# Sending the bf16 parts of q and k to DRAM in three steps instead of one, in a fused two-layer transformer block

## The chip, the cores and the metric

One Trainium2 chip, one core. The metric is the device time of one execution in microseconds (us). The change is written in Bass: every engine has an instruction list of its own, in a fixed order, and waits are semaphore waits written by hand.

## The reference

The input is x of 16 batches x 512 tokens x 128 channels in f32. Four residual layers follow one another, each with a layer norm in front (scale and shift free):

```
x = x + attention0(layernorm(x))     # 16 heads of 8, q, k, v with bias, softmax(q k^T / sqrt(8)) v, then wo
x = x + gated_mlp(layernorm(x))      # silu(x wg) * (x wu), 384 wide, then wd; weights from int8 ranges
x = x + attention1(layernorm(x))     # 16 heads of 8, q and k RMS-normalised per head, softmax, projection
x = x + moe_lora(layernorm(x))       # base linear + softmax-gated sum of 8 rank-8 experts, times 2
```

Per batch and attention layer there are 16 heads x 512 x 512 scores, each a dot product over 8 numbers only.

## The kernel before, in words

**The attention trick.** A score's dot product is over 8 numbers in f32. The kernel splits each f32 q and k into three bf16 parts (part 0 = q rounded to bf16, part 1 = the rest rounded, part 2 = the rest of that) and multiplies six pairs of parts (`Q_PART`, `K_PART`), so that 8 x 6 = 48 rows of bf16 stand for one head's f32 product. Two more rows hold the negated row maximum in two bf16 parts, so that the exponential needs no separate subtraction. To get parts, heads and terms onto the right partitions, the parts go through DRAM: SP writes `q_rows` and `k_rows` (L437), three DMAs for each of q and k, for terms 0 to 2, 3 and 4, and 5; then SP reads them back, four heads' worth at a time, into `q_stack` and `k_stack` (L452).

**Where the parts are made.** ScalarE (ACT) takes q and k out of PSUM (`take_qk`, L771) and makes part 0 (`take_part0`, a copy on L718, tiles qp and kp). GpSimd (POOL) makes part 1 (L602, then L604 updates the rest) and part 2 (L610). Semaphores `part0`, `resid1` and `part2` tell of them. ACT may overwrite part 0 only when the last batch's rows have landed (`rows_out`).

**Staging.** The kernel is one software pipeline. Every (layer, batch) attention is a slot of 64 units; there are 32 slots, in the order (0,0), (0,1), (0,2), (1,0), (0,3), (1,1), (0,4), (1,2), ... In each unit t TensorE (PE) makes one attention score tile (`attend_score`, L1237), one tile for the row maxima of the attention 26 units later (`max_score`, L1227), and each fourth unit four probability-times-value products (L1252). VectorE (DVE) reduces the maximum tile (L973), ACT takes the exponential (L742). Everything else (norms, projections, the MLP) is hung into this grid at units given in tables (`PE_AT`, `ACT_AT`, `DVE_AT`, `POOL_AT`, `SP_AT`): a name, and a unit counted from a slot's start. PE's tiles are handed PSUM banks from two rings: `A_RING` (banks 0, 1, 2, 7: all scores, all maxima and most pieces) and `V_RING` (3, 4, 5: two pieces, `xt3` and `kt`); bank 6 collects the attention output.

**The tables set order, not time.** Each engine walks the units in order and does what is due. SP has no work of its own in a unit: it runs ahead until a wait stops it, and all that is listed later waits behind that. SP's work, by its due units in a slot: `rows0` to `rows3` (`max_rows`, L458: two small DMAs that put the maxima of a quarter into `q_stack`; attention score 16n of the slot waits for quarter n), `den`/`rden` (L464, L472, L478: softmax denominators out and their reciprocals back in), `lx` (`load_x`, L418: the input of a later batch, which DVE reads first, L949), `lr0`, `cpx2`, `store`, `half0`/`half1` (`stack_half`, L452), and `out_p0`/`out_p1` (`parts_out`, L437: all six row DMAs of layer 0's or layer 1's next batch, three after q's part 2 is there and three after k's).

**Where the rows stand.** For layer 0 and batches 3 to 15 the group `P0` is used (`out_p0` at unit 47 of the slot of (0, b-1), 8 later for b = 3), for batches 1 and 2 the group `P0_fast` (unit 17; for b = 2, unit 19). Batch 0 goes ahead of the loop. Layer 1 has `out_p1` at unit 21 of the slot before (1, b), in most cases shifted 2 earlier. When two things are due in the same unit, their order in SP's loop decides.

Of the kernel before, what the change touches and what calls it, by code (L numbers as in the profile page):

```python
# [12 lines left out]
BATCH, SEQ, D = 16, 512, 128  # L13
# [11 lines left out]
PARTS = 3  # L25
TERMS = 6
Q_PART = (0, 0, 0, 1, 1, 2)
K_PART = (0, 1, 2, 0, 1, 0)
# [47 lines left out]
SP_AT = {"A": {"rows0": -5, "rows1": 9, "rows2": 32, "rows3": 43, "den0": 40, "rden0": 52, "den1": 71,  # L76
                "rden1": 74},
         "P0": {"out_p0": 47, "half0_p0": 72, "half1_p0": 95},
         "P0_fast": {"out_p0": 17, "half0_p0": 37, "half1_p0": 60},
         "S0": {"lx": 16},  # L80
         "M1": {"lr0": 52},
         "M2": {"out_p1": 21},
         "H1": {"cpx2": -16, "half0_p1": 38, "half1_p1": 42},
         "H1_tail": {"cpx2": 45, "half0_p1": 35, "half1_p1": 66},
         "E": {"store": 91}}
# [32 lines left out]
PE_DUE, ACT_DUE, DVE_DUE, POOL_DUE, SP_DUE = (due_table([t]) for t in (PE_AT, ACT_AT, DVE_AT, POOL_AT, SP_AT))  # L118
# [5 lines left out]
def at(due, name, t):  # L124

    return due[name][t] if name in due and t in due[name] else None
# [72 lines left out]
def build(nc, T, out_dram):  # L199
    ctx = ExitStack()  # L200
    with ctx:
# [7 lines left out]
        q_rows = [nc.dram_tensor(f"q_rows{l}", (128, TERMS, SEQ), BF16).ap() for l in (0, 1)]  # L209
        k_rows = [nc.dram_tensor(f"k_rows{l}", (128, TERMS, SEQ), BF16).ap() for l in (0, 1)]  # L210
# [173 lines left out]
        def _(sp):  # L384
            def hold(sem, value):
                need(sp, sem, value)
# [37 lines left out]
            load_res0(0)  # L424
            load_x(1)

            def parts_out(l, which, b):

                for n in which:
                    rows, pick = ((q_rows[l], Q_PART), (k_rows[l], K_PART))[n]  # L430
                    for h in (0, 1):
                        hold(stack_in[l][h], 64 * b)
                    hold(first_in[l], 64 * b)
                    hold(part2[2 * l + n], b + 1)
                    for j0, j1 in ((0, 3), (3, 5), (5, 6)):
                        step = pick[j0 + 1] - pick[j0] if j1 - j0 > 1 else 0
                        sp.dma_start(rows[:, j0:j1, :],  # L437
                                     bass.AP(qp[l][n][:, :, :].tensor, pick[j0] * SEQ,
                                             [[PARTS * SEQ, 128], [step * SEQ, j1 - j0], [1, SEQ]])
                                     ).then_inc(rows_out[l][n], 16)  # L440

            def stack_half(l, half, b):
                for n in (0, 1):
# [47 lines left out]
                sp.dma_start(out_dram[b:b + 1].rearrange("a (t p) d -> p (a t) d", p=128), x3[:, :, :]  # L491
                             ).then_inc(stored, 16)

            parts_out(0, (0, 1), 0)
            hold(k_ones, 1)
            stack_half(0, 0, 0)
            stack_half(0, 1, 0)
            for t in TIMES:
                b = at(SP_DUE, "half1_p0", t)
                if b is not None:  # L500
                    stack_half(0, 1, b)
                b = at(SP_DUE, "lx", t)
                if b is not None:
                    load_x(b)
                a = at(SP_DUE, "den1", t)
                if a is not None:
                    den_lines(a[0], 1, a[1])
                a = at(SP_DUE, "rows1", t)
                if a is not None:
                    max_rows(a[0], 1, a[1])  # L510
                a = at(SP_DUE, "rden1", t)
                if a is not None:
                    rden_lines(a[0], 1, a[1])
                b = at(SP_DUE, "lr0", t)
                if b is not None and b + 1 < BATCH:
                    load_res0(b + 1)
                b = at(SP_DUE, "out_p1", t)
                if b is not None:
                    parts_out(1, (0, 1), b)
                a = at(SP_DUE, "rows2", t)  # L520
                if a is not None:
                    max_rows(a[0], 2, a[1])
                b = at(SP_DUE, "half0_p1", t)
                if b is not None:
                    if b == 0:
                        hold(k_ones, 2)
                    stack_half(1, 0, b)
                b = at(SP_DUE, "half1_p1", t)
                if b is not None:
                    stack_half(1, 1, b)  # L530
                b = at(SP_DUE, "out_p0", t)
                if b is not None:
                    parts_out(0, (0, 1), b)
                a = at(SP_DUE, "den0", t)
                if a is not None:
                    den_lines(a[0], 0, a[1])
                a = at(SP_DUE, "rows3", t)
                if a is not None:
                    max_rows(a[0], 3, a[1])
                b = at(SP_DUE, "cpx2", t)  # L540
                if b is not None:
                    copy_x2(b)
                b = at(SP_DUE, "half0_p0", t)
                if b is not None:
                    stack_half(0, 0, b)
                a = at(SP_DUE, "rden0", t)
                if a is not None:
                    rden_lines(a[0], 0, a[1])
                a = at(SP_DUE, "rows0", t)
                if a is not None:  # L550
                    max_rows(a[0], 0, a[1])
                b = at(SP_DUE, "store", t)
                if b is not None:
                    store(b)
# [849 lines left out]
```

## Time and profile before

| | us |
|---|---|
| median of 3 runs | 1800.41 |
| lowest, highest run | 1794.83, 1801.01 |
| the profiled execution, its own time | 1797.05 |
| span in its profile, first to last instruction | 1795.3 |
| mean granted TensorE clock | 0.982 of full |
| PE busy | 1684.5 (94%) |
| DVE busy | 1543.6 (86%) |
| ACT busy | 1415.8 (79%) |
| POOL busy | 586.6 (33%) |
| DMA, 16 engines, mean share of the SP queue | 27.6% |

The profile tells of one execution. Times in its rows count from the first instruction. A timeline row has start, length, engine, source line, tiles written and read, a count when neighbours are merged, and in brackets the idle time just before it with what ended it. SPq rows are DMA issues: their length is the time SP spends on issuing, not the transfer. PEld rows are TensorE's weight loads, at which a score's wait shows.

### The profile page before, as it was taken

The numbers are of one execution on the slowest core, as the hardware profiler recorded it, in microseconds if no ns is written. First come the engines' busy times: TensorE is split into PE (matmuls) and PEld (weight loads), VectorE is DVE, ScalarE is ACT, GpSimd is POOL, SyncE is SP. The second block draws the span as 40 slices with busy tenths as digits, with TensorE's granted clock in tenths as the row PEclk, the third lists the DMA queues.
The fourth block names the chain that finished last, engine by engine and source line by source line (L and its number), as shares of the span: only waits on it lengthen the run. The fifth ranks groups of instructions, "written<-read, shape, count | busy, mean of one in ns | idle before, by whom it ended". The sixth has DMA issues, their size and how long they took to land.

```text
span 1795.3 us, 32451 instructions
## 1 busy us (share of the span) xinstructions
PE 1684.5 (94%) x10962; PEld 633.9 (35%) x10962; DVE 1543.6 (86%) x3347; ACT 1415.8 (79%) x2922; POOL 586.6 (33%) x840
## 2 busy tenths in 40 slices
PE   5999999999999999999999999999999999999995
PEld 2233333434333343333334333343433334334333
DVE  4988899898898989889898989989899898887981
ACT  2778788787978878787887988878797887777872
POOL 4224234151423324233242423415142332423311
PEclk8899999999999999999999999999999999999996
DMA  5232414223142322404232140422314142122310
GB/s 121 67 85 71 116 38 120 68 83 104 32 121 55 121 61 73 114 27 129 58 114 66 56 128 24 120 71 79 104 32 120 55 121 55 46 59 78 87 36 25
DMA packets 164024, 140.97 MB, mean 79 GB/s; under 512 B 40778, under 2 KB 145428, under 8 KB 163860
## 3 DMA queue, kind: packets, MB, share of 16 engines
q1 hardware_dynamic: 162084, 137.92, 27.6%
q8 instruction: 88, 1.44, 0.3%
q10 hardware_dynamic: 1776, 0.98, 0.2%
q14 instruction: 76, 0.62, 0.1%
HBM read 76.99 MB, written 55.57 MB: 74 GB/s over the span
## 4 chain that ended last, share of the span: by engine, by line
PE 62%; DVE 29%; issue 3%; ACT 2%; DMA 2%; SPq 1%; POOL 1%; DVEq 0%; ACTq 0%; POOLq 0%
DVE neg_max L973 20%; PE ps L1252 19%; PE ps L1237 14%; PE ps L1227 8%; PE ps L1273 7%; PE ps L1184 5%; PE ps L1266 3%; PE ps L1317 3%; DVE bn L949 2%; PE ps L1278 2%; DVE x L1010 2%; PE ps L1323 2%; DVE neg_high L979 1%; ACT probs L742 1%; DVE mv L957 1%
## 5 line engine op out<-in xcount | busy, mean ns | idle before, releaser
L973 DVE TENSOR_REDUCE neg_max<-ps 128x1 f32<-128x512 f32 x2048 | 1299.8, 682 | 100.2 <-PE ps L1227 91.1
L742 ACT ACTIVATE probs<-ps 128x512 f32<-128x512 f32 x2048 | 1093.3, 600 | 232.7 <-PE ps L1237 230.4
L1227 PE MATMUL ps<-k_stack,q_stack 48*128 48x512 bf16 x2048 | 679.1, 388 | 42.9 <-DVE neg_max L973 31.9
L1237 PE MATMUL ps<-q_stack,k_stack 50*128 50x512 bf16 x2048 | 632.1, 383 | 7.6 <-ACT probs L742 3.1
L1252 PE MATMUL ps<-probs,v_aug 128*32 128x512 f32 x4096 | 548.5, 608 | 0.7 <-ACT o_raw L718 0.7
L1237 PEld LDWEIGHTS ps<-q_stack,k_stack 50*128 50x128 bf16 x2048 | 148.1, 94 | 530.0 <-ACT probs L742 249.4
L1227 PEld LDWEIGHTS ps<-k_stack,q_stack 48*128 48x128 bf16 x2048 | 153.4, 93 | 227.4 <-DVE neg_max L973 202.1
L595 POOL TENSOR_TENSOR rstd<-vpe,half_neg 128x4 f32<-128x4 f32 x64 | 64.5, 1009 | 351.6 <-DVE vpe L964 351.5
L647 POOL TENSOR_TENSOR ht<-up,gs 128x512 f32<-128x512 f32 x48 | 61.1, 1273 | 223.2 <-ACT up L718 223.2
L1252 PEld LDWEIGHTS ps<-probs,v_aug 128*32 128x32 f32 x4096 | 80.7, 108 | 143.2 <-issue 73.7
L748 ACT ACTIVATE xn<-x,shift,rstd 128x128 f32<-128x128 f32 x192 | 80.7, 486 | 37.8 <-POOL shift L597 37.8
L616 POOL TENSOR_TENSOR o_raw<-o_raw,rden_all 128x512 f32<-128x512 f32 x64 | 81.3, 1270 | 49.9 <-DMA rden_all<-rden_rows 49.4
L602 POOL TENSOR_TENSOR qp<-qf,qp 128x512 bf16<-128x512 f32 x32 | 37.0, 1157 | 165.0 <-ACT qp L718 165.0
L654 POOL TENSOR_TENSOR coef<-gating,rm 128x64 f32<-128x64 bf16 x64 | 16.7, 292 | 225.3 <-DVE gating L1073 225.3
L1278 PE MATMUL ps<-wo,o_raw 128*128 128x128 f32 x512 | 67.3, 286 | 8.7 <-POOL o_raw L616 7.9
L626 POOL TENSOR_TENSOR nw_t<-nw_y 128x128 f32<-128x128 f32 x48 | 19.1, 399 | 156.2 <-DVE nw_y L1045 153.8
L1278 PEld LDWEIGHTS ps<-wo,o_raw 128*128 128x128 f32 x512 | 61.2, 196 | 18.3 <-issue 12.0
L1022 DVE SCALAR_TENSOR_TENSOR gs<-th,ps 128x512 f32<-128x512 f32 x48 | 32.7, 682 | 35.3 <-POOL ht L647 35.3
L1184 PE MATMUL ps<-ident,xn 128*128 128x128 f32 x256 | 44.1, 298 | 17.1 <-ACT xn L748 16.7
L718 ACT ACTIVATE up<-ps 128x512 f32<-128x512 f32 x48 | 28.7, 597 | 37.0 <-PE ps L1273 36.9
L1273 PE MATMUL ps<-xnt,w_up 128*128 128x256 f32 x192 | 54.3, 405 | 0.5 <-DVE gs L1022 0.5
L1010 DVE TENSOR_TENSOR x<-ps,x 128x512 f32<-128x512 f32 x32 | 22.0, 688 | 37.3 <-PE ps L1317 21.6
(117 smaller groups left out, 1579.5 us busy)
## 6 DMA issues: line engine op xcount, KB each, us to landing
rden_all<-rden_rows SPq DMA_DIRECT2D x64, 256.0 KB
q_rows<-qp SPq DMA_DIRECT2D x32, 384.0 KB, 2.9
k_rows<-kp SPq DMA_DIRECT2D x32, 384.0 KB, 2.9
q_stack<-q_rows SPq DMA_DIRECT2D x64, 192.0 KB, 3.8
k_stack<-k_rows SPq DMA_DIRECT2D x64, 192.0 KB, 4.8
q_stack<-q_rows SPq DMA_DIRECT2D x64, 144.0 KB, 2.9
k_stack<-k_rows SPq DMA_DIRECT2D x64, 144.0 KB, 3.3
q_rows<-qp SPq DMA_DIRECT2D x32, 256.0 KB, 3.1
```

What stands on the lines that cost most here:

```text
L595: pool.tensor_tensor(rstd[k][:, :], vpe[k][:, :], half_neg[:, :], ALU.pow).then_inc(rstd_ready[k], 1)
L616: pool.tensor_tensor(o_of(l, b)[:, c, :], o_of(l, b)[:, c, :], rden_all[:, c, :], ALU.mult).then_inc(att_ready[l], 1)
L647: pool.tensor_tensor(ht[:, c, :], up[:, :], gs[:, :], ALU.mult).then_inc(ht_done, 1)
L742: act.activation(probs[:, g % RING, :], home("score", (l, b, u)), ACT.Exp).then_inc(exps, 1)
L748: last = act.activation(xn[k][:, t, :], x[:, t, :], ACT.Identity, bias=shift[k][:, t:t + 1], scale=rstd[k][:, t:t + 1])
L973: dve.tensor_reduce(neg_max[l][:, pair // 2, col:col + 1], home("max", (l, b, n)), AX.X, ALU.max, negate=True).then_inc(max_taken, 1)
L1184: return pe.transpose(dst, src, ident[0:n, 0:n])
L1227: pe.matmul(home("max", (l, b, m)), q_stack[l][row:row + KROWS, pair, tok:tok + 128], k_stack[l][row:row + KROWS, pair, :], start=True, st ...
L1237: pe.matmul(home("score", (l, b, u)), k_stack[l][row:row + AROWS, pair, tok:tok + 128], q_stack[l][row:row + AROWS, pair, :], start=True, ...
L1252: last = pe.matmul(acc[32 * j:32 * j + 32, :], v_of(l, b)[:, kt, 8 * e + 2 * group + pp, :], probs[:, (g + j) % RING, :], start=(s == 0 an ...
L1273: return pe.matmul(dst[:, 256 * half:256 * half + 256], w, xt[:, 256 * half:256 * half + 256], start=True, stop=True)
L1278: last = pe.matmul(by_tile(dst)[:, t, :], o_of(l, b)[:, c, 128 * t:128 * t + 128], wo[l][:, c, :], start=c == 0, stop=c == 1)
```

## The change

Each of the three pairs of row DMAs now has its own call and its own waits. `first_rows` sends what needs part 0 alone (terms 0 to 2 of q, term 5 of k), `second_rows` what needs part 1 (terms 3 and 4 of both), `third_rows` what is left (term 5 of q, terms 0 to 2 of k, all three parts). The number of DMAs, their sizes and the semaphore they count on stay. In layer 0 the three calls stand at units 31, 38 and 47 (`P0`) and 8, 12 and 17 (`P0_fast`); in layer 1 all three stand at unit 21, where `out_p1` was.

```diff
--- before.py
+++ after.py
@@ -75,11 +75,11 @@
            "E": {"nf3": 32, "mix": 48}}
 SP_AT = {"A": {"rows0": -5, "rows1": 9, "rows2": 32, "rows3": 43, "den0": 40, "rden0": 52, "den1": 71,
                 "rden1": 74},
-         "P0": {"out_p0": 47, "half0_p0": 72, "half1_p0": 95},
-         "P0_fast": {"out_p0": 17, "half0_p0": 37, "half1_p0": 60},
+         "P0": {"rows_a0": 31, "rows_b0": 38, "rows_c0": 47, "half0_p0": 72, "half1_p0": 95},
+         "P0_fast": {"rows_a0": 8, "rows_b0": 12, "rows_c0": 17, "half0_p0": 37, "half1_p0": 60},
          "S0": {"lx": 16},
          "M1": {"lr0": 52},
-         "M2": {"out_p1": 21},
+         "M2": {"rows_a1": 21, "rows_b1": 21, "rows_c1": 21},
          "H1": {"cpx2": -16, "half0_p1": 38, "half1_p1": 42},
          "H1_tail": {"cpx2": 45, "half0_p1": 35, "half1_p1": 66},
          "E": {"store": 91}}
@@ -424,20 +424,37 @@
             load_res0(0)
             load_x(1)
 
-            def parts_out(l, which, b):
-
-                for n in which:
-                    rows, pick = ((q_rows[l], Q_PART), (k_rows[l], K_PART))[n]
-                    for h in (0, 1):
-                        hold(stack_in[l][h], 64 * b)
-                    hold(first_in[l], 64 * b)
-                    hold(part2[2 * l + n], b + 1)
-                    for j0, j1 in ((0, 3), (3, 5), (5, 6)):
-                        step = pick[j0 + 1] - pick[j0] if j1 - j0 > 1 else 0
-                        sp.dma_start(rows[:, j0:j1, :],
-                                     bass.AP(qp[l][n][:, :, :].tensor, pick[j0] * SEQ,
-                                             [[PARTS * SEQ, 128], [step * SEQ, j1 - j0], [1, SEQ]])
-                                     ).then_inc(rows_out[l][n], 16)
+            def rows_of(l, n, j0, j1):
+                rows, pick = ((q_rows[l], Q_PART), (k_rows[l], K_PART))[n]
+                step = pick[j0 + 1] - pick[j0] if j1 - j0 > 1 else 0
+                sp.dma_start(rows[:, j0:j1, :],
+                             bass.AP(qp[l][n][:, :, :].tensor, pick[j0] * SEQ,
+                                     [[PARTS * SEQ, 128], [step * SEQ, j1 - j0], [1, SEQ]])
+                             ).then_inc(rows_out[l][n], 16)
+
+            def first_rows(l, b):
+
+                for h in (0, 1):
+                    hold(stack_in[l][h], 64 * b)
+                hold(first_in[l], 64 * b)
+                hold(part0[l], 2 * b + 1)
+                rows_of(l, 0, 0, 3)
+                hold(part0[l], 2 * b + 2)
+                rows_of(l, 1, 5, 6)
+
+            def second_rows(l, b):
+
+                hold(resid1[2 * l], 2 * b + 1)
+                rows_of(l, 0, 3, 5)
+                hold(resid1[2 * l + 1], 2 * b + 1)
+                rows_of(l, 1, 3, 5)
+
+            def third_rows(l, b):
+
+                hold(part2[2 * l], b + 1)
+                rows_of(l, 0, 5, 6)
+                hold(part2[2 * l + 1], b + 1)
+                rows_of(l, 1, 0, 3)
 
             def stack_half(l, half, b):
                 for n in (0, 1):
@@ -491,7 +508,9 @@
                 sp.dma_start(out_dram[b:b + 1].rearrange("a (t p) d -> p (a t) d", p=128), x3[:, :, :]
                              ).then_inc(stored, 16)
 
-            parts_out(0, (0, 1), 0)
+            first_rows(0, 0)
+            second_rows(0, 0)
+            third_rows(0, 0)
             hold(k_ones, 1)
             stack_half(0, 0, 0)
             stack_half(0, 1, 0)
@@ -514,9 +533,15 @@
                 b = at(SP_DUE, "lr0", t)
                 if b is not None and b + 1 < BATCH:
                     load_res0(b + 1)
-                b = at(SP_DUE, "out_p1", t)
-                if b is not None:
-                    parts_out(1, (0, 1), b)
+                b = at(SP_DUE, "rows_a1", t)
+                if b is not None:
+                    first_rows(1, b)
+                b = at(SP_DUE, "rows_b1", t)
+                if b is not None:
+                    second_rows(1, b)
+                b = at(SP_DUE, "rows_c1", t)
+                if b is not None:
+                    third_rows(1, b)
                 a = at(SP_DUE, "rows2", t)
                 if a is not None:
                     max_rows(a[0], 2, a[1])
@@ -528,9 +553,15 @@
                 b = at(SP_DUE, "half1_p1", t)
                 if b is not None:
                     stack_half(1, 1, b)
-                b = at(SP_DUE, "out_p0", t)
-                if b is not None:
-                    parts_out(0, (0, 1), b)
+                b = at(SP_DUE, "rows_a0", t)
+                if b is not None:
+                    first_rows(0, b)
+                b = at(SP_DUE, "rows_b0", t)
+                if b is not None:
+                    second_rows(0, b)
+                b = at(SP_DUE, "rows_c0", t)
+                if b is not None:
+                    third_rows(0, b)
                 a = at(SP_DUE, "den0", t)
                 if a is not None:
                     den_lines(a[0], 0, a[1])
```

## Rows read from the trace of the kernel before

**Rows 1.** The page: engines' busy time, and the chain that ended last, by engine

```profile
PE 1684.5 (94%) x10962; PEld 633.9 (35%) x10962; DVE 1543.6 (86%) x3347; ACT 1415.8 (79%) x2922; POOL 586.6 (33%) x840
...
PE 62%; DVE 29%; issue 3%; ACT 2%; DMA 2%; SPq 1%; POOL 1%; DVEq 0%; ACTq 0%; POOLq 0%
```

**Rows 2.** Waits of the weight loads: us in total, times, longest

```profile
PEld ps L1237 <- DMA q_stack<-m_parts: 6.0, 7, 1.0
```

**Rows 3.** Timeline of SP, 54 to 70 us

```profile
54.96 1.27 SPq L458 DMA_DIRECT2D q_stack<-m_parts  x2
56.27 0.40 SPq L418 DMA_DIRECT2D x_in<-in_L_attn_x  x1
```

**Rows 4.** Timeline of ACT, 57 to 63 us

```profile
61.35 0.66 ACT L718 ACTIVATE kp<-kf 128x512 bf16<-128x512 f32 x1
```

**Rows 5.** Timeline of PE, 54 to 72 us

```profile
61.27 0.39 PE L1237 MATMUL ps<-q_stack,k_stack 50*128 50x512 bf16 x1
```

**Rows 6.** Timeline of POOL, 20 to 130 us

```profile
62.08 1.15 POOL L602 TENSOR_TENSOR kp<-kf,kp 128x512 bf16<-128x512 f32 x1 [0.27 <-ACT kp L718]
...
111.06 1.16 POOL L602 TENSOR_TENSOR kp<-kf,kp 128x512 bf16<-128x512 f32 x1
```

**Rows 7.** Timeline of DVE, 54 to 72 us

```profile
64.13 0.48 DVE L949 BATCH_NORM_STATS2 bn<-x_in 128x6 f32<-128x128 f32 x2
```

**Rows 8.** DMA issues of the whole run: KB each, median us to landing

```profile
x_in<-in_L_attn_x SPq DMA_DIRECT2D x16, 256.0 KB, 4.0
```

**Rows 9.** Line L418 from 56 to 57 us: the one load of x_in there

```profile
DMA to landing us min/median/max: 2.8/2.8/2.8
```

**Rows 10.** Timeline of SP, 101 to 121 us

```profile
104.64 0.64 SPq L478 DMA_DIRECT2D rden_all<-rden_rows  x1
105.33 0.46 SPq L418 DMA_DIRECT2D x_in<-in_L_attn_x  x1
```

**Rows 11.** Timeline of ACT, 98 to 122 us

```profile
108.56 0.63 ACT L718 ACTIVATE kp<-kf 128x512 bf16<-128x512 f32 x1
```

**Rows 12.** Timeline of DVE, 98 to 126 us

```profile
110.03 0.47 DVE L949 BATCH_NORM_STATS2 bn<-x_in 128x6 f32<-128x128 f32 x2
...
112.62 0.69 DVE L1010 TENSOR_TENSOR x<-ps,res 128x512 f32<-128x512 f32 x1 [1.52 <-PE ps L1278]
```

**Rows 13.** Timeline of SP, 1020 to 1050 us

```profile
1027.54 1.32 SPq L437 DMA_DIRECT2D k_rows<-kp  x3
1029.66 1.28 SPq L458 DMA_DIRECT2D q_stack<-m_parts  x2
...
1041.08 1.30 SPq L458 DMA_DIRECT2D q_stack<-m_parts  x2
```

**Rows 14.** Timeline of ACT, 1028 to 1032 us

```profile
1030.01 0.61 ACT L718 ACTIVATE kp<-kf 128x512 bf16<-128x512 f32 x1
```

**Rows 15.** Timeline of weight loads, 1033 to 1036 us

```profile
1034.20 0.09 PEld L1237 LDWEIGHTS ps<-q_stack,k_stack 50*128 50x128 bf16 x1 [0.84 <-issue]
```

**Rows 16.** Timeline of SP, 176 to 198 us

```profile
177.38 1.99 SPq L437 DMA_DIRECT2D k_rows<-kp  x3
179.41 1.31 SPq L458 DMA_DIRECT2D q_stack<-m_parts  x2
```

**Rows 17.** Timeline of weight loads, 181 to 183 us

```profile
181.87 0.09 PEld L1237 LDWEIGHTS ps<-q_stack,k_stack 50*128 50x128 bf16 x1 [0.99 <-DMA q_stack<-m_parts]
```

**Rows 18.** Timeline of SP, 718 to 728 us

```profile
721.28 1.30 SPq L458 DMA_DIRECT2D q_stack<-m_parts  x2
```

**Rows 19.** Timeline of weight loads, 725 to 727 us

```profile
726.38 0.09 PEld L1237 LDWEIGHTS ps<-q_stack,k_stack 50*128 50x128 bf16 x1 [0.84 <-DMA q_stack<-m_parts]
```

**Rows 20.** Timeline of weight loads, 1695 to 1697 us

```profile
1696.14 0.09 PEld L1227 LDWEIGHTS ps<-k_stack,q_stack 48*128 48x128 bf16 x1 [0.52 <-DMA k_stack<-k_rows]
```

**Rows 21.** Stretches of 2 us: length, busy us (count) of PE, PEld, DVE, ACT, POOL, clock, DMA

```profile
115.00:117.00 2.00, 1.24 (x5) 0.39 (x5) 1.97 (x6) 0.68 (x2) 1.20 (x2) 1.00 0.78 301
117.00:119.00 2.00, 2.00 (x8) 0.41 (x11) 2.00 (x4) 2.00 (x7) 0.00 (x0) 0.53 0.31 102
```

## The prediction, made before the changed kernel was run

> **What bounds the kernel now.** I read the page first. TensorE is busy 94% of the span, DVE 86%, and the chain that ended last is PE for 62% and DVE for 29% [rows 1]. In it DMA has 2% and SP's issues 1%. So the two compute engines hand the work to and fro, and a transfer costs time only where PE or DVE stands still for it. The list of waits says how seldom that is: the scores' weight loads waited for the row maxima that SP sends (m_parts) 7 times, 6.0 us in all [rows 2], out of 128 sendings (32 slots, four quarters). The rows that the change moves are hardly waited for. So a gain can be small only, and the question is what the moved DMAs, and above all their waits, do to what stands behind them in SP's list. For that I went through SP's timeline slot by slot and set each item's gate beside its consumer.
>
> **What is the same.** Each batch and layer still has six row DMAs of the same sizes; nothing is added on ACT, POOL, DVE or PE. SP issues as many, at 0.44 us each (1.32 us for three [rows 13]).
>
> **Where the change adds a wait.** In the loop `first_rows` waits for part 0 of k, `second_rows` for part 1 of k. SP is in order. So I look at what lies between the old place and the new ones.
>
> *Slot 0, batch 1 (`P0_fast`, units 8, 12, 17).* Before, SP sends rows1 (unit 9) at 54.96 and the load of x for batch 2 (unit 16) at 56.27 [rows 3], both ahead of the row DMAs. After, both stand behind waits. Part 0 of k is finished by ACT at 61.35 + 0.66 = 62.01 [rows 4]; this copy stands at unit 15, ahead of the stall, and isn't itself delayed. Then SP issues k's first row DMA (0.44) and rows1 (1.27), done at 63.8. From issue's end to release m_parts take about 1.15 us: issued by 179.41 + 1.31 = 180.72, released the load at 181.87 [rows 16, 17]. So the score of unit 16, which began at 61.27 [rows 5], can begin at 65.0: PE stands still for 3.7 us, once. The load of x comes later still: `second_rows` waits for POOL's first operation on k, 62.08 + 1.15 = 63.23 [rows 6], which is past by then, so two more issues, and the load goes at 64.9. Landing takes 2.8 us in the one case where nothing was in flight [rows 9] and 4.0 in the median [rows 8]; with 512 KB of rows just ahead I take the median: 68.9 to 69.0. DVE reads x at 64.13 now [rows 7], in unit 19, in order before the next maxima. It loses 4.8 us. PE's 3.7 us lie inside this, not on top, for both end at the same place. **Term 1: +4.8.** Bounds: 3.7 (PE's stall alone) to 5.5.
>
> *Slot 1, batch 2 (units 74, 78, 83).* rows1 is at 73 and safe. But the load of x for batch 3 stands at unit 80, ahead of the old place and behind `second_rows`. It goes at 105.33 now, right behind the denominators [rows 10]. After: part 0 of k is ready at 108.56 + 0.63 = 109.19 [rows 11], then POOL's part 1 of k at 111.06 + 1.16 = 112.22 [rows 6]; two issues around it, and the load goes at about 112.75, landing after 4.0 at 116.75. DVE wants it at 110.03 [rows 12], so it stands for 6.7 us. Some of this is free: right after, DVE waits 1.52 us for PE's projection anyway before it adds at 112.62 [rows 12], and PE has that ready while DVE stands. 6.7 - 1.5 = 5.2. **Term 2: +5.2.** Bounds: 4 (landing in 2.8) to 6.7 (nothing absorbed).
>
> *The load of x in all later slots* stands at unit 16 of the other kind of slot, with no row DMA before it. No change.
>
> *Even slots from batch 4 on, 12 times (units 31, 38, 47).* `first_rows` at 31 is just ahead of rows2 at 32. Part 0 of k is done at 1030.01 + 0.61 = 1030.62 [rows 14], while rows2 goes at 1029.66 now [rows 13]. After: k's DMA (0.44), then rows2 (1.28) up to 1032.4, usable at 1033.55. Its score begins at 1034.20 [rows 15]. 0.65 us of the 2.1 us of slack are left. So rows2 is late by 1.5 us, and this costs nothing, as long as PE's own time to unit 32 covers it; if that cover goes, each 0.1 us costs 1.2 in all. `second_rows` at 38 comes before den0, half1 and rows3. Its data are ready some tenths before den0's gate, so its two issues (0.9 us) push these by at most 0.9, I take 0.4. Rows3 has the least room of all: issued until 721.28 + 1.30 = 722.58 [rows 18], it lands within the last 0.84 us before the score at 726.38 [rows 19]. Seven scores at most have so little room [rows 2]. **Term 3: +0.5**, bounds 0 and 7 x 0.9 = 6.3.
>
> *Layer 1 (unit 21).* All three stand where one did, q's and k's first two pairs go out while POOL still works, and after the last wait SP has one issue instead of three: 0.9 us earlier. This reaches PE only where the stack load came last, in the last slot but one: 0.52 us before 1696.14 [rows 20]. **Term 4: -0.5**, bounds -1 and 0.
>
> **The clock.** At 115 to 117 PE was busy 1.24 of 2.00 us, and in the next 2 us the granted clock was 0.53, close to its 1.2 GHz level [rows 21]. A stall of 3.7 us in slot 0 may bring such a stretch where there is none now. I put it at 0, since DVE stands for x until 69 anyway and PE catches up meanwhile; upper bound 1 us a stall (2 us at 0.53 of the clock lose 0.9). The Trainium skill (TensorE: Matmul & The Clock Gate, HAM oscillation) charges a throttled stretch with half its length each time PE stood idle too long; the row agrees that a lull comes before the fall. By that rule the sum would be 1 us higher.
>
> **The sum.** 4.8 + 5.2 + 0.5 - 0.5 = +10.0 us. The profiled execution took 1797.05 (1.75 around its span of 1795.3); that gives 1807.1. The median of the runs shown is 3.4 above it, so on the median's footing 1800.4 + 10.0 = 1810.4. Nothing later wins this back: every slot is gated by its own PE and DVE work, not by a date.
>
> **Rivals.**
> *A. The steady slots pay (0.20).* Rows2 lands behind k's 128 KB, rows3 behind 512 KB more in flight. Rows3, sent behind stack loads, takes from 722.58 to past 725.5 [rows 18, 19], nearly 2 us more than the 1.15 of rows2. If rows2 became like that, 12 x (1.5 to 2.0 less the 0.65 of slack) would add 10 to 16 us: 1820 to 1827. Against it: at 179.41 rows2 went right behind three row DMAs (1.99 us of issue) and was usable 1.15 us later [rows 16, 17], so row DMAs don't hold it up. The Trainium skill (DMA: Bandwidth & Descriptors, Queues, rings and completion order) says that an engine consumes a ring's descriptors in order, by which m_parts must queue behind whatever was issued before; the trace speaks for it behind stack loads and against it behind row writes.
> *B. The early stalls are swallowed (0.15).* If x were read later than its row says, or if the start were bound by something that goes on meanwhile (POOL, SP), one of terms 1 and 2 falls: +5, 1805.5. Against it: in both places DVE was busy right up to that read, with no idle time in its row [rows 7, 12].
> *C. Not slower (0.05).* The place is SP's list in the layer 1 group and behind rows3: rows sent in pieces leave the DMA engines less crowded when rows3 and the stack loads go. Rows3 was last 7 times [rows 2]; winning all 6.0 us, the 0.5 at the end and losing only half of the early stalls gives -1.5: 1799. It decides only if the releases for rows3 were true stalls. In the rows seen they fall inside a pause of 0.84 us that also appears with no DMA [rows 15], so there is little to win.
> *D. It doesn't do what it says.* Only if rows_a waited for nothing; its waits are constants that reach part 0 of k, so this has no share of its own.
>
> **How the numbers follow.** The forecast case has 0.60, its own range is 1806.5 to 1814 (the bounds of terms 1, 2 and the clock). About 0.5% (9 us) is what a measurement of this kernel can tell from no change, and 10.0 lies just beyond it. Of the forecast case I count 0.39 above 9 us and 0.21 below; A is slower (0.20, together 0.59); B and C are the same, but for the 0.04. Faster by 9 us has no mechanism, 0.04 is for what I don't see. So slower 0.59, same 0.37, faster 0.04. The range: 1803 takes in B, 1823 half of A; C and the rest of A are left out.
>
> **What the changed profile would show.** Right: SP's m_parts near 62.5 instead of 54.96, a PE idle of 3 to 4 us ended by DMA m_parts near 61 to 65, DVE's batch-norm reads of x_in waiting some 4 to 7 us for the load, twice, and from batch 4 on a constant offset of about 10 us with slots as long as before. Wrong: waits for m_parts growing with the batches (A), an offset under 5 us at 130 us (B), or a period that is shorter (C).

## The result, and the profile after

| | before | after |
|---|---|---|
| median, us | 1800.41 (5 runs, 1794.83 to 1801.01) | 1807.77 (5 runs, 1806.78 to 1809.54) |
| profiled execution's span | 1795.3 | 1806.0 |
| ratio to before | 1 | 1.0048, 95% interval 1.0034 to 1.0061 |
| mean granted TensorE clock | 0.982 | 0.978 |

The kernel is slower: 0.0048 of 1800.4 is 8.6 us, with the interval's ends at 6 and 11; the medians themselves lie 7.4 apart. The interval leaves out 1, but the ratio is just under the 0.5% that the prediction had set as its bound. The page's two lines that answer to [rows 1], busy time by engine and the shares of the chain:

```profile
PE 1688.9 (94%) x10962; PEld 634.1 (35%) x10962; DVE 1541.5 (85%) x3347; ACT 1417.5 (78%) x2922; POOL 587.7 (33%) x840
...
PE 62%; DVE 28%; issue 3%; ACT 2%; DMA 2%; SPq 1%; POOL 1%; DVEq 0%; ACTq 0%; POOLq 0%
```

PE's busy time has grown by 4.4 us and DVE's has shrunk by 2.1 against [rows 1], while the span is 10.7 longer: most of what was added is idle time. Where it is, the starts of the slots tell. For every run below I read from the trace when the first attention score of slots 0, 1, 2, 4 and 28 starts, and list the lengths between them (us), with the stretches that began in slots 0 and 1 in which the granted clock was 0.5, that is at the 1.2 GHz level. Left out of that column is the one that is already on when slot 0 begins, and ends some 9 us later (at 55.7 in both kernels' first profiles); four runs (before_again, after_again, x9, x10) have no record of it, but their value products at 53.4 us take 1.93 us like those of the others there. Slot lengths and stretches are of one execution each, the ratio is of all executions of a run.

| run | slot 0 | slot 1 | 2 and 3 | 4 to 27 | 28 to end | at 1.2 GHz, from (for) | ratio to before (95%) |
|---|---|---|---|---|---|---|---|
| before | 46.9 | 61.4 | 107.4 | 1279.3 | 254.3 | 117 (3.4) | |
| before_again | 46.3 | 64.6 | 107.2 | 1279.3 | 253.5 | 118 (10.2) | one execution |
| **after** | **52.1** | **65.8** | 107.7 | 1279.4 | 254.2 | 66 (6.8), 124 (6.8) | 1.0048 (1.0034 to 1.0061) |
| after_again | 52.5 | 65.6 | 107.8 | 1280.6 | 254.6 | 67 (6.8), 125 (6.8) | one execution |
| x1_fast_undone | 46.7 | 60.8 | 107.2 | 1280.4 | 254.0 | none | 1.0009 (0.9996 to 1.0023) |
| x2_batch1_only | 50.6 | 63.0 | 106.1 | 1278.5 | 256.8 | 63 (6.8), 121 (6.8) | 1.0031 (1.0020 to 1.0042) |
| x3_batch2_only | 46.3 | 67.0 | 107.8 | 1281.6 | 254.8 | 116 (10.2) | 1.0037 (1.0020 to 1.0053) |
| x4_x_first | 52.4 | 62.0 | 107.6 | 1280.3 | 254.5 | 65 (6.8), 123 (3.4) | 1.0022 (1.0010 to 1.0034) |
| x5_steady_undone | 52.0 | 65.6 | 108.2 | 1279.3 | 254.4 | 65 (6.8), 123 (6.8) | 1.0038 (1.0023 to 1.0053) |
| x6_rows1_first | 50.1 | 61.5 | 107.4 | 1279.7 | 254.2 | 69 (3.4), 120 (3.4) | 1.0013 (1.0001 to 1.0024) |
| x7_waits_alone | 51.8 | 65.1 | 107.5 | 1279.7 | 257.0 | 65 (6.8), 120 (10.2) | 1.0040 (1.0027 to 1.0053) |
| x8_four_more_issues | 46.8 | 65.2 | 107.5 | 1300.2 | 256.1 | 117 (10.2) | 1.0136 (1.0121 to 1.0152) |
| x9_clean | 46.4 | 61.3 | 111.6 | 1280.2 | 254.8 | 118 (3.4) | 1.0020 (1.0009 to 1.0030) |
| x10_layer1_only | 47.1 | 64.7 | 107.2 | 1279.6 | 254.1 | 119 (10.2) | 1.0002 (0.9993 to 1.0011) |

After against before: slot 0 +5.2, slot 1 +4.4, all the rest together +0.3; the first score starts 0.8 us later (46.92 against 46.12), which isn't the change's doing, as the two repeats both start it at 47.8. The loss is in the first two slots.

It has two parts, and slots 0 and 1 as stretches show them (columns: length; busy us and counts of PE, PEld, DVE, ACT, POOL; granted clock; DMA share; GB/s). Before:

```profile
46.12:92.98 46.86, 45.39 (x265) 12.25 (x264) 42.53 (x86) 38.44 (x78) 9.35 (x9) 0.90 0.21 65
92.98:154.42 61.44, 57.26 (x365) 22.63 (x362) 49.99 (x113) 47.87 (x98) 16.73 (x17) 0.97 0.27 75
```

The changed kernel:

```profile
46.92:99.00 52.08, 47.52 (x267) 12.18 (x265) 42.80 (x86) 38.60 (x78) 9.34 (x9) 0.85 0.20 58
99.00:164.79 65.79, 58.46 (x364) 22.56 (x360) 49.87 (x113) 47.93 (x98) 16.74 (x17) 0.95 0.26 71
```

PE's idle time (length less busy) grew by 3.1 us in each of the two slots, and PE took 2.1 and 1.2 us longer for the same work, at a lower mean clock.

SP's timeline of the changed kernel in slot 0 (answers to [rows 3]; start, length, engine and line, tiles, count):

```profile
58.73 0.39 SPq L430 DMA_DIRECT2D q_rows<-qp  x1
62.45 0.34 SPq L430 DMA_DIRECT2D k_rows<-kp  x1
62.84 1.28 SPq L475 DMA_DIRECT2D q_stack<-m_parts  x2
64.17 0.40 SPq L430 DMA_DIRECT2D q_rows<-qp  x1
64.61 0.47 SPq L430 DMA_DIRECT2D k_rows<-kp  x1
65.12 0.44 SPq L418 DMA_DIRECT2D x_in<-in_L_attn_x  x1
```

rows1 (m_parts) goes at 62.84 instead of 54.96, right behind k's first row DMA, which waited for kp. x goes at 65.12 instead of 56.27. PE's timeline of the changed kernel from 60 to 76 us (the bracket is the idle time ahead of the row and what ended it):

```profile
60.69 1.06 PE L1283 MATMUL ps<-probs,v_aug 128*32 128x512 f32 x8
65.34 0.39 PE L1268 MATMUL ps<-q_stack,k_stack 50*128 50x512 bf16 x1 [3.59 <-DMA q_stack<-m_parts]
...
67.08 1.93 PE L1283 MATMUL ps<-probs,v_aug 128*32 128x512 f32 x8
...
70.91 1.93 PE L1283 MATMUL ps<-probs,v_aug 128*32 128x512 f32 x8
```

And DVE's, of the same kernel, from 59 to 76 us:

```profile
65.80 2.48 DVE L1004 TENSOR_REDUCE neg_max<-ps 128x1 f32<-128x512 f32 x4 [3.69 <-PE ps L1258]
68.61 0.49 DVE L980 BATCH_NORM_STATS2 bn<-x_in 128x6 f32<-128x128 f32 x2 [0.33 <-DMA x_in<-in_L_attn_x]
69.62 1.29 DVE L1004 TENSOR_REDUCE neg_max<-ps 128x1 f32<-128x512 f32 x2 [0.52 <-PE ps L1258]
```

PE stands idle for 3.59 us until m_parts have landed. When it goes on, its eight value products (L1283, eight of 32 columns) take 1.93 us twice, against 1.06 at 60.69, at the full clock: the fall of the clock. DVE waits 0.33 us for x only, because its own four maxima had waited 3.69 us for PE, and then 0.52 us for PE again. The changed kernel's stretches of 2 us (columns as above):

```profile
64.00:66.00 2.00, 0.66 (x6) 0.31 (x7) 0.20 (x1) 0.24 (x1) 1.92 (x2) 0.99 0.50 160
66.00:68.00 2.00, 2.00 (x12) 0.30 (x9) 2.00 (x4) 1.83 (x4) 0.00 (x0) 0.50 0.91 256
...
70.00:72.00 2.00, 2.00 (x12) 0.30 (x9) 1.97 (x6) 1.66 (x4) 0.00 (x0) 0.50 0.00 0
72.00:74.00 2.00, 2.00 (x13) 0.42 (x9) 1.17 (x3) 0.80 (x2) 0.00 (x0) 0.81 0.00 0
```

The first row has PE busy 0.66 of 2 us: the lull in which the stall lies. The clock is at 1.2 GHz (0.50) in the rows up to 72, and the last row has both levels in it. The issue order of SP in slot 1 of the changed kernel (answers to [rows 10]):

```profile
110.82 0.65 SPq L495 DMA_DIRECT2D rden_all<-rden_rows  x1
...
114.99 0.33 SPq L430 DMA_DIRECT2D k_rows<-kp  x1
...
118.68 0.32 SPq L430 DMA_DIRECT2D k_rows<-kp  x1
119.05 0.43 SPq L418 DMA_DIRECT2D x_in<-in_L_attn_x  x1
```

The reciprocals (L495) go at 110.82. Each of k's two row DMAs stands for its wait, until 114.99 and 118.68, and only then x goes, at 119.05; before it went right behind the reciprocals. DVE's timeline there (answers to [rows 12]):

```profile
122.09 0.49 DVE L980 BATCH_NORM_STATS2 bn<-x_in 128x6 f32<-128x128 f32 x2 [6.21 <-DMA x_in<-in_L_attn_x]
...
123.08 0.68 DVE L1041 TENSOR_TENSOR x<-ps,res 128x512 f32<-128x512 f32 x1
```

DVE stands 6.21 us for x. The add (L1041) that before waited 1.52 us for PE follows without any wait: that much was free.

### The profile page after: what moved, and what is told of

Same layout as the page of the kernel before. It is cut to its first block, busy times and chain, and to the rows that moved or that the text cites. A ratio compares the mean times of both kernels' runs of the same rounds, so it can differ in the third digit from the quotient of the medians.

```text
span 1806.0 us, 32391 instructions
## 1 busy us (share of the span) xinstructions
PE 1688.9 (94%) x10962; PEld 634.1 (35%) x10962; DVE 1541.5 (85%) x3347; ACT 1417.5 (78%) x2922; POOL 587.7 (33%) x840
## 4 chain that ended last, share of the span: by engine, by line
PE 62%; DVE 28%; issue 3%; ACT 2%; DMA 2%; SPq 1%; POOL 1%; DVEq 0%; ACTq 0%; POOLq 0%
DVE neg_max L1004 19%; PE ps L1283 19%; PE ps L1268 14%; PE ps L1258 8%; PE ps L1304 7%; PE ps L1215 5%; PE ps L1297 3%; PE ps L1348 3%; DVE bn L980 2%; DVE x L1041 2%; PE ps L1309 2%; PE ps L1354 2%; ACT probs L773 1%; DVE neg_high L1010 1%; DVE mv L988 1%
## 5 line engine op out<-in xcount | busy, mean ns | idle before, releaser
L1283 PE MATMUL ps<-probs,v_aug 128*32 128x512 f32 x4096 | 551.4, 611 | 0.8 <-ACT o_raw L749 0.7
L626 POOL TENSOR_TENSOR rstd<-vpe,half_neg 128x4 f32<-128x4 f32 x64 | 64.6, 1010 | 357.3 <-DVE vpe L995 357.2
L1283 PEld LDWEIGHTS ps<-probs,v_aug 128*32 128x32 f32 x4096 | 80.8, 108 | 144.3 <-issue 73.9
L647 POOL TENSOR_TENSOR o_raw<-o_raw,rden_all 128x512 f32<-128x512 f32 x64 | 81.5, 1273 | 53.4 <-DMA rden_all<-rden_rows 53.1
L1041 DVE TENSOR_TENSOR x<-ps,x 128x512 f32<-128x512 f32 x32 | 22.0, 688 | 37.3 <-PE ps L1348 21.6
```

The lines of the kernel that those rows point to most:

```text
L626: pool.tensor_tensor(rstd[k][:, :], vpe[k][:, :], half_neg[:, :], ALU.pow).then_inc(rstd_ready[k], 1)
L647: pool.tensor_tensor(o_of(l, b)[:, c, :], o_of(l, b)[:, c, :], rden_all[:, c, :], ALU.mult).then_inc(att_ready[l], 1)
L1283: last = pe.matmul(acc[32 * j:32 * j + 32, :], v_of(l, b)[:, kt, 8 * e + 2 * group + pp, :], probs[:, (g + j) % RING, :], start=(s == 0 an ...
```

## The experiments

Three theories stood at the start. **Order of waits:** in slots 0 and 1 urgent things stand behind waits that the change put ahead of them. **Steady slots:** the twelve later slots lose a little each (rival A of the prediction). **Traffic:** the row transfers themselves, earlier and in pieces, hold up what lands behind them. A fourth came with the first profile: **the clock** adds to a stall what the stall itself doesn't show. Diffs are against the changed kernel; its tables stand in one line each.

**x1_fast_undone.** Batches 1 and 2 at the old place.

```diff
-         "P0_fast": {"rows_a0": 8, "rows_b0": 12, "rows_c0": 17, ...
+         "P0_fast": {"rows_a0": 17, "rows_b0": 17, "rows_c0": 17, ...
```

> Rows of batches 1 and 2 sent at the old place (all three steps at unit 17), steady slots as changed. Waits-in-order theory: no wait of PE or DVE for a load in slots 0 and 1, offset against the kernel before under 0.5 us at the end of slot 1, the whole kernel 0 to 1 us above the one before (ratio 0.999 to 1.002). Rival, the steady slots pay: the ratio stays above 1.003, with the offset growing from slot 4 on.

Measured: ratio 1.0009, slot 0 -0.2 and slot 1 -0.6 us against before. The loss in slots 0 and 1 is gone, though the steady slots are as changed. The interval (0.9996 to 1.0023) leaves room for no loss and for one of 4 us; the profiled execution is the fastest of its ten (1796.7, median 1802.9). Slot 1 is even shorter than before, and this is the one execution of all without a slow stretch there.

**x2_batch1_only** and **x3_batch2_only.** Only one of the two batches has units 8 and 12, the other has 17. The diff is x2's; in x3 the two lines R1 and R2 have each other's units.

```diff
+         "R1": {"rows_a0": 8, "rows_b0": 12, "rows_c0": 17},
+         "R2": {"rows_a0": 17, "rows_b0": 17, "rows_c0": 17},
...
+    if early:
+        GROUPS.append((f"R{b}", b, SLOT_OF[0, b - 1], (0, 0, 2)[b]))
```

> Only batch 1's rows early (units 8 and 12), batch 2's at 17. Waits-in-order theory: slot 0 grows by 5.2 us as in the changed kernel, slot 1 by nothing; ratio near 1.003. If the two losses depend on each other (the second stall is there only because the first one moved the transfers), slot 1 behaves as before here too and the third run shows no loss at all.

> Only batch 2's rows early, batch 1's at 17. Waits-in-order theory: slot 0 unchanged, slot 1 grows by 4.4 to 5.5 us, DVE waits about 6 us for x of batch 3. Sum of the two growths of this run and the last is that of the changed kernel (9.6 us) within 1 us. Rival, dependent losses: less than 2 us here.

Measured: x2 slot 0 +3.7, slot 1 +1.6; x3 slot 0 -0.6, slot 1 +5.6. Each batch brings its own loss, and the two sum to 10.3 over slots 0 and 1 where the changed kernel has 9.6 (by the ratios to 0.68%, where it has 0.48%, which the intervals can't tell apart). But the sizes miss in a way that needed a reason: x2's stall is the changed kernel's (3.57 us), its slot 0 is 1.5 us shorter, and its slot 1 grew with nothing changed in it. PE's timeline of x2 in slot 0:

```profile
63.47 0.60 PE L1272 MATMUL ps<-q_stack,k_stack 50*128 50x512 bf16 x1 [3.57 <-DMA q_stack<-m_parts]
...
65.43 1.93 PE L1287 MATMUL ps<-probs,v_aug 128*32 128x512 f32 x8
...
69.26 1.20 PE L1287 MATMUL ps<-probs,v_aug 128*32 128x512 f32 x8
```

Here the clock had fallen already when PE went on (its first score takes 0.60, not 0.39), and was back before the second group of products had ended (1.20). 0.7 us of the slow stretch, which the trace has from 62.8 on, lay in the idle time. More comes from the stretch that was on when slot 0 began: it ended 6.4 us into the slot here and 8.8 in the changed kernel. PE's idle time in slot 0 is 4.6 us in both runs, its busy time 46.0 against 47.5: the whole 1.5 us is busy time, and so is nearly all that slot 1 grew by (PE busy 58.7 for 57.3, with 6.8 us at 1.2 GHz for 3.4).

**x4_x_first.** The loads of x for batches 2 and 3 at unit 7, ahead of all waits.

```diff
-         "S0": {"lx": 16},
+         "LX": {"lx": 16},
+         "LX_early": {"lx": 7},
...
-    GROUPS.append(("S0", b, max(SLOT_OF[0, b - 2] + (b > 3), b - 2), 0))
+    for group in ("S0", "LX_early" if b < 4 else "LX"):
+        GROUPS.append((group, b, max(SLOT_OF[0, b - 2] + (b > 3), b - 2), 0))
```

> The row DMAs as in the changed kernel, but the loads of x for batches 2 and 3 stand at unit 7, ahead of the waits. Waits-in-order theory: no wait of DVE for x; slot 1 loses nothing, slot 0 still has PE's 3.6 us wait for rows1 and the slow clock behind it, so it grows by 4 to 5 us; the whole 4 to 5.5 us above the kernel before. Rival, DMA traffic: x lands late through the row transfers in flight, wherever it is issued, and slot 1 still loses over 2 us.

Measured: slot 1 +0.6, where the changed kernel has +4.4: the loss of slot 1 was x, with the longer slow stretch that came with it (3.4 us here, as before, for 6.8). Slot 0 +5.5, over the 4 to 5 expected, and as much as with x late. PE's timeline of x4 in slot 0:

```profile
64.61 0.39 PE L1270 MATMUL ps<-q_stack,k_stack 50*128 50x512 bf16 x1 [3.55 <-DMA q_stack<-m_parts]
...
66.35 1.94 PE L1285 MATMUL ps<-probs,v_aug 128*32 128x512 f32 x8
```

And DVE's:

```profile
67.47 0.48 DVE L982 BATCH_NORM_STATS2 bn<-x_in 128x6 f32<-128x128 f32 x2
```

PE has stood 3.55 us and its value products take 1.94 again. DVE reads x at 67.47 with no wait, and slot 0 is no shorter for it. The traffic theory has nothing left in slot 1, where the row transfers are the changed kernel's.

**x6_rows1_first.** As x2, batch 1 alone, with its first step behind rows1 (unit 9) and still ahead of x.

```diff
+         "R1": {"rows_a0": 10, "rows_b0": 12, "rows_c0": 17},
+         "R2": {"rows_a0": 17, "rows_b0": 17, "rows_c0": 17},
```

> Batch 1 only: its first step at unit 10, behind rows1 (9), its second at 12, ahead of the load of x (16). So PE gets rows1 in time and x is late. Theory that x sets slot 0 (the prediction's term 1): slot 0 grows by 4 to 4.8 us, with DVE waiting 3.5 to 4.5 us for x. Theory that PE's stall and the slow clock behind it set slot 0: under 4 us, and what there is shows as DVE's wait for x with no fall of the clock.

DVE's timeline of x6 in slot 0:

```profile
66.51 0.49 DVE L984 BATCH_NORM_STATS2 bn<-x_in 128x6 f32<-128x128 f32 x2 [2.55 <-DMA x_in<-in_L_attn_x]
```

And PE's:

```profile
67.65 0.39 PE L1262 MATMUL ps<-k_stack,q_stack 48*128 48x512 bf16 x1 [3.02 <-DVE neg_max L1008]
67.97 1.16 PE L1287 MATMUL ps<-probs,v_aug 128*32 128x512 f32 x8
...
71.31 1.49 PE L1287 MATMUL ps<-probs,v_aug 128*32 128x512 f32 x8
```

Measured: slot 0 +3.2, less than the 4 to 4.8 of the first theory and less than PE's stall gives. DVE waits 2.55 us for x, not 3.5 to 4.5, and PE idles 3.02 us in turn, until DVE's maxima (neg_max) free a bank. Against my second clause the clock did fall, but for 3.4 us only: a late x costs too, by DVE, and with less of the slow clock.

**x7_waits_alone.** The waits without the DMAs: for batches 1 and 2 the waits stay at 8 and 12; all six row DMAs go at 17, as before.

```diff
-                rows_of(l, 0, 0, 3)
+                wait_alone = l == 0 and b in (1, 2)
+                if not wait_alone:
+                    rows_of(l, 0, 0, 3)
                 hold(part0[l], 2 * b + 2)
...
```

> Batches 1 and 2: SP waits at units 8 and 12 as changed, but all six row DMAs go at unit 17 as before. If the waits cost the time, slots 0 and 1 grow by 8 to 9.6 us (the x loads go 0.9 us earlier without two issues ahead). If the row transfers and their issues cost it, they grow by less than 2 us.

Measured: slot 0 +4.9, slot 1 +3.7, together 8.6. The waits cost it: no row DMA is moved in these slots, and nearly the whole loss is there, with a ratio of 1.0040 for 1.0048. In slot 0 this is plain (PE idle 4.4 us in it, for 1.5 before). In slot 1 DVE waited 4.92 us for x, but the slow stretch was of 10.2 us, and before_again, which has such a stretch and no change, is nearly as long there (64.6 for 65.1): this trace alone doesn't show what the wait cost in slot 1.

**x5_steady_undone.** The reverse of x1: layer 0's steady slots at the old place.

```diff
-         "P0": {"rows_a0": 31, "rows_b0": 38, "rows_c0": 47, ...
+         "P0": {"rows_a0": 47, "rows_b0": 47, "rows_c0": 47, ...
```

> Batches 1 and 2 early as changed, layer 0's rows from batch 3 on back at unit 47 in one place. Waits-in-order theory: the loss is all in slots 0 and 1 (9.6 us), and stays 9 to 10.5 us; ratio near 1.005 like the changed kernel. Rival, the steady slots pay: the ratio falls to that of slots 0 and 1 alone while the waits for m_parts fall from 23 to 7, and the end of the kernel comes over 1 us earlier than in the changed one.

Measured: waits of the scores for m_parts fall from 23 to 6, and slots 4 to 27 take 1279.3 against 1279.4. The steady slots cost nothing that shows; over the runs of the table (x8 aside) these 24 slots scatter from 1278.5 to 1281.6, and the ratio, 1.0038, can't be told from the changed kernel's. The list of waits of the changed kernel's weight loads (us in total, times, longest; answers to [rows 2]):

```profile
PEld ps L1268 <- DMA q_stack<-m_parts: 23.1, 23, 4.5
```

The same line of x5:

```profile
PEld ps L1268 <- DMA q_stack<-m_parts: 8.8, 6, 4.5
```

The 17 waits more come to 14.3 us, 0.84 each: the pause that stands before such a score without any DMA, too [rows 15]. The list calls them waits for m_parts because these land within the pause. They tell how little slack is left, not what is lost.

**x8_four_more_issues.** How much slack it was: batches 1 and 2 at 17, and four spare DMAs (64 KB each, into memory that nothing reads) behind k's first row DMA, ahead of rows2, in each of the twelve steady slots.

```diff
                 rows_of(l, 1, 5, 6)
+                if l == 0 and b >= 4:
+                    for n in range(4):
+                        sp.dma_start(spare[4 * b + n], ident[:, :]).then_inc(spared, 16)
```

> Batches 1 and 2 at the old place; in the 12 steady slots four more 64 KB DMAs (4 x 0.44 = 1.76 us of issue) go between the first step and rows2, so rows2 is usable some 3.3 us later than before. Slack theory: 2.1 us were there, so each slot loses 1.1 to 1.3 us, 13 to 16 us in all, seen as waits for m_parts over 1.5 us in 12 places. Rival, PE's wait is made up for by work queued behind (DVE and ACT catch up): under 6 us.

SP's timeline of x8 in one such slot, and behind it the weight load that waits for rows2:

```profile
504.69 1.88 SPq L448 DMA_DIRECT2D spare<-ident  x4
506.62 1.29 SPq L480 DMA_DIRECT2D q_stack<-m_parts  x2
```

```profile
509.06 0.09 PEld L1274 LDWEIGHTS ps<-q_stack,k_stack 50*128 50x128 bf16 x1 [1.89 <-DMA q_stack<-m_parts]
```

Measured: in slots 4 to 27 +21 us, 1.75 a slot, above the 13 to 16 expected. The wait shown bears out the slack: 1.89, less the pause of 0.84, is 1.05 us of true stall, where 1.1 to 1.3 were expected, and the four issues took 1.88, so 0.8 us of them were hidden, near the 0.65 of the prediction. Of the twelve such waits ten are of 1.9 to 2.1 us, two of 2.8 and 3.4; all twelve, less the pause, come to 15.3 us. What is more, 5.6 us, goes with the clock: PE is busy 6.2 us longer in these slots than in the changed kernel (1239.1 for 1232.9), and the trace has five stretches at 1.2 GHz there, 24 us in all, where the changed kernel has none.

**x9_clean.** Three steps, each behind the urgent item next to it (rows2 at 32, rows3 at 43).

```diff
-         "P0": {"rows_a0": 31, "rows_b0": 38, "rows_c0": 47, ...
-         "P0_fast": {"rows_a0": 8, "rows_b0": 12, "rows_c0": 17, ...
+         "P0": {"rows_a0": 33, "rows_b0": 44, "rows_c0": 47, ...
+         "P0_fast": {"rows_a0": 17, "rows_b0": 17, "rows_c0": 17, ...
```

> Three steps kept, but placed where nothing urgent stands behind a wait: batches 1 and 2 all at 17, later ones at 33 (behind rows2), 44 (behind rows3) and 47. Waits-in-order theory: waits for m_parts back to about 7, no loss in slots 0 and 1; ratio 0.998 to 1.001, so neither faster nor slower. A gain beyond 0.3% would mean that sending in steps helps where it holds nothing up.

Measured: 1.0020, against expectation. The loss is 4.2 us in slots 2 and 3. Batch 3 is shifted by 8, so its first step stood at unit 41, between den0 and half1. SP's timeline of x9 there:

```profile
187.71 0.38 SPq L430 DMA_DIRECT2D q_rows<-qp  x1
188.13 0.48 SPq L430 DMA_DIRECT2D k_rows<-kp  x1
188.71 1.03 SPq L469 DMA_DIRECT2D q_stack<-q_rows  x2
189.78 1.00 SPq L469 DMA_DIRECT2D k_stack<-k_rows  x2
190.83 1.29 SPq L475 DMA_DIRECT2D q_stack<-m_parts  x2
```

The weight load that waits for these m_parts:

```profile
195.94 0.09 PEld L1268 LDWEIGHTS ps<-q_stack,k_stack 50*128 50x128 bf16 x1 [2.79 <-DMA q_stack<-m_parts]
```

And x9's stretches of 2 us:

```profile
190.00:192.00 2.00, 2.00 (x16) 0.53 (x16) 2.00 (x6) 1.36 (x4) 2.00 (x2) 1.00 1.09 230
...
198.00:200.00 2.00, 2.00 (x12) 0.18 (x6) 0.89 (x2) 0.43 (x1) 0.00 (x0) 0.50 0.66 187
```

The same rows3 before the change, its issue and the weight load that it releases:

```profile
188.63 1.30 SPq L458 DMA_DIRECT2D q_stack<-m_parts  x2
```

```profile
193.05 0.09 PEld L1237 LDWEIGHTS ps<-q_stack,k_stack 50*128 50x128 bf16 x1 [0.84 <-DMA q_stack<-m_parts]
```

SP waited for nothing here, but rows3 was late in its list: ACT had m_parts ready at 189.54 in the trace, and rows3 goes at 190.83, once the two row DMAs and half1's four loads are issued. Before, it went at 188.63, as soon as ACT had them (188.61). That is 1.3 us. The transfer was slower too: m_parts release the score at 195.94, 3.8 us after the end of their issue at 192.12, with the DMA share at 1.09 from 190 to 192, where the same took at most 3.1 us before (189.93 to 193.05), behind the stack loads alone, and rows2 behind row DMAs alone 1.15 [rows 16, 17]. PE itself idles 1.9 us (the weight load's 2.79 less the pause of 0.84), and the row from 198 on has the clock at 0.50: of the 4.2 us in slots 2 and 3, 3.6 are longer busy time of PE (103.3 for 99.7). So the order of issues has its part here too, beside the traffic; no run separates the two. In the changed kernel batch 3's first step stands one item earlier, at unit 39, ahead of den0, and no such stall shows.

**x10_layer1_only.** Layer 0's rows all at the old places.

```diff
+         "P0": {"rows_a0": 47, "rows_b0": 47, "rows_c0": 47, ...
+         "P0_fast": {"rows_a0": 17, "rows_b0": 17, "rows_c0": 17, ...
```

> Only layer 1's rows in steps; layer 0's all at the old place. The prediction's term 4: -0.5 us, seen as the wait for the stack load in slot 30 gone, ratio 0.999 to 1.0005. A rival that layer 1's earlier SP costs time: ratio over 1.001.

Measured: 1.0002. Of the maxima's four waits for stack loads before (one of them is [rows 20]) three are left, 2.9 us for 3.9. Nothing that can be told from no change.

**before_again** and **after_again.** Both kernels once more, with no edit, one execution each.

> The kernel before once more, for the spread of one kernel's slots. Clock theory: slot 1 has a slow stretch of 0, 3.4, 6.8 or 10.2 us here too, and its length against the first profile moves by about half the difference of these stretches (0 for the same stretch, -0.7 for none, +1.5 to 3.7 for more). If slot 1 varies without that, the clock is not its reason.

> The changed kernel once more. Slot 0 grows by 3.6 us (PE's stall) plus half of what of the slow stretch lies behind the stall: 5.2 with a stretch from 65 to 72, 3.7 with one from 62 on. Slot 1 grows by 4 to 5.5 us.

Measured, first in a stretch of 2 us of slot 1, before:

```profile
122.00:124.00 2.00, 2.00 (x14) 0.62 (x12) 2.00 (x4) 2.00 (x5) 0.00 (x0) 1.00 0.00 0
```

The same stretch of before_again, and the whole of its slot 1:

```profile
122.00:124.00 2.00, 2.00 (x11) 0.56 (x9) 0.73 (x2) 1.30 (x3) 0.00 (x0) 0.50 0.01 2
94.10:158.66 64.56, 60.02 (x364) 23.26 (x361) 49.98 (x113) 48.09 (x98) 16.77 (x17) 0.92 0.26 72
```

One program, two profiles: in the first the clock is full from 122 to 124, in the second it is 0.50, and slot 1 is 3.1 us longer, within the 1.5 to 3.7 expected; PE's busy time has 2.8 of it (60.02 for 57.26). Over all runs that changed nothing in slot 1 its length goes with the slow stretch: 60.8 with none (x1), 61.3 to 61.5 with 3.4 us (before, x6, x9), 63.0 with 6.8 (x2), 64.6 to 65.2 with 10.2 (before_again, x8, x10). From 60.8 to 64.8 over 10.2 us that is some 0.4 us for each us at 1.2 GHz. PE's busy time in the slot rises alike, 55.9, 57.0 to 57.3, 58.7 and 60.0 us, for the same work. No run forced the clock there, so that the one brings the other is read from what goes together. after_again has slots 0 and 1 at 52.5 and 65.6, that is 5.6 and 4.2 above the first profile of before, where 5.2 and 4 to 5.5 were expected.

## Why the prediction was right, and where it wasn't

*Which way, and where.* Slower, by the waits ahead of rows1 and x in slots 0 and 1, each once, nothing won back: borne out by x1 (waits gone, loss gone), x2 and x3 (each its own), x4 (x alone for slot 1) and x7 (waits alone). The median, 1807.8, lies in the range, 2.6 below the forecast of 1810.4. The case with the largest chance (0.59), slower by over 0.5%, is missed narrowly, with 0.48% and an interval on both sides of the bound.

*Term 1, slot 0: +4.8, measured +5.2.* The size was right and the mechanism wrong. "PE's 3.7 us lie inside this" made x the setter. x4 took x away and slot 0 stayed at +5.5. PE's stall of 3.6 set it: of the 5.2, PE's idle time has 3.1 and its longer busy time, in the slow clock behind the stall, 2.1 (3.3 and 2.2 in x4). x landed 3.5 us after its issue, and DVE waited 0.33 for it, where 4.8 were forecast. That 4.8 is close to 5.2 is luck. x6 shows the other mechanism alone: with rows1 in time, the late x costs 3.2.

*Term 2, slot 1: +5.2, measured +4.4.* DVE's wait was 6.2 for 6.7, the free 1.5 us were there, and x4, with x early, leaves 0.6. So the wait was read rightly, but not what it costs. Of the 4.4, PE's idle time has 3.1, and 1.2 is its longer busy time, with 6.8 us at 1.2 GHz where before had 3.4. Against slots that nothing changed and that had as long a slow stretch, the late x costs less: 2.8 against x2 (65.8 for 63.0), 2.4 in x3 against before_again (67.0 for 64.6), 0.5 in x7. Against before_again the changed kernel's slot grew by 1.2 only. What DVE's wait alone costs stays open between these: a stall of DVE moves the stretch of slow clock too.

*The clock: put at 0, with 1 us as the bound.* This step failed. Its reason was that DVE stands for x until 69 and PE catches up meanwhile; DVE stood 0.33 us. Measured, 6.8 us at 1.2 GHz went with 2.1 us more of PE's busy time in slot 0, and the 3.4 us more than before in slot 1 with 1.2 us (in the unchanged slots it is some 0.4 for each us). Together that is 3.3 us where nothing was put down. The Trainium skill (TensorE: Matmul & The Clock Gate, HAM oscillation) counts half of the throttled time as lost, by which an estimate for 6.8 us is 3.4: the right direction, and more than the runs show. Why they show less wasn't tried.

*The footing: the profile's sum put on the median.* Against its own profile the sum is close: 10.0 forecast, 10.7 measured between the two profiled spans. In part this is luck. The 10.7 are 6.2 us of PE's idle time in the two slots, 3.3 of its busy time, 0.8 by which the first score is later and 0.3 elsewhere; the 10.0 were all standing time. Between the medians it is 7.4. The prediction took the 3.4 us from the profiled execution to the median as a plain offset. before_again has 3.1 us of just such a difference inside slot 1, at the place of term 2. If other executions of before have it too, they hold already some of what the change brings, and adding the whole sum to the median counts it twice; the single times don't tell.

*Term 3, steady slots: +0.5, measured +0.1, within the scatter of these slots.* The list of waits names m_parts more often, as they now land inside PE's pause, and x5 shows no time behind it. x8 bears out the slack (0.8 for 0.65). Rival A's own picture, m_parts held up by transfers ahead, costs time in x9 alone, behind row writes and stack loads together, and even there a later issue had its part.

*Term 4, layer 1: -0.5.* The wait of [rows 20] is gone from x10's trace; by x10's ratio the time can't be told from none.

## What to carry to other kernels

On an in-order issuing engine a send moved earlier carries its wait with it: list what stands between the new and the old place, and when each must land; in a steady state slack may hide it, in the pipeline's first slots, where tables are squeezed, it does not. A stall of the matmul engine cost its length plus what the slow clock behind it took, here 2 us behind 3.6; and when a before-profile has a slow stretch at the place that a change touches, look at a second profile before putting a price on it.

## What the runs showed that was not expected

Part of a kernel's own scatter (1794.8 to 1801.0) has a place: at 117 us the clock falls for 3.4 or for 10.2 us in two executions of one program, 3.1 us apart in that slot. And the time of the small m_parts DMAs from issue's end to release depends on what was issued before them: 1.15 us behind three row DMAs [rows 16, 17], at most 3.1 us behind stack loads (before, 189.93 to 193.05), 3.8 us behind row DMAs and four stack loads (x9).
